# A small memset on POOL behind each gather, in message passing and the last layer

## The reference

```
for _ in range(3):
    msgs = relu(take(h, src) @ W_edge + b_edge)
    agg  = segment_sum(msgs, dst, num_segments=50000)
    h    = relu(concatenate([agg, h]) @ W_agg + b_agg)
x = layernorm(x + h)
```

## Time and profile before

| | us |
|---|---|
| timed runs, median of 3 | 5096.5 (5095.79 to 5099.93) |
| profiled execution, span | 6166.6 |
| of it message passing, two rounds | about 1717 |
| last layer | about 1222 |
| attention | about 1294 |
| feed-forward | about 996 |
| POOL busy over the span | 3168.2 (51%) |
| PE busy over the span | 4568.4 (74%) |

### The profile page before, as it was taken

One profiled execution on the slowest core, in us unless ns is written; L12 is line 12 of the kernel. 1 busy time (PEld: TensorE's weight loads), 2 busy tenths in 40 slices (PEclk: granted clock), 3 DMA queues, 4 the chain that ended last, 5 costly groups with the idle time before them and its releaser, 6 DMA issues. The chain is left out here.

```text
span 6166.6 us, 106939 instructions
## 1 busy us (share of the span) xinstructions
PE 4568.4 (74%) x21995; PEld 2882.5 (47%) x21996; DVE 3657.1 (59%) x12075; ACT 2092.9 (34%) x4610; POOL 3168.2 (51%) x3348
## 2 busy tenths in 40 slices
PE   5666657777767777688888887566666666888887
PEld 3444435555555555555555554344444443333333
DVE  7666643333333333466666655677777776777777
ACT  0222223333333333322323323222222223666665
POOL 1555554444344444333333332666666664888887
PEclk9888878888888888889999998555555556999999
DMA  0333335555545555455665655333333332333333
GB/s 26 128 129 127 124 123 150 149 151 152 152 146 151 149 151 149 144 172 174 187 189 174 187 176 156 86 90 88 92 90 88 90 88 69 107 103 106 104 103 96
DMA packets 690049, 789.03 MB, mean 128 GB/s; under 512 B 145529, under 2 KB 545648, under 8 KB 689900
## 3 DMA queue, kind: packets, MB, share of 16 engines
q1 hardware_dynamic: 577004, 568.56, 28.9%
q0 software_dynamic: 112896, 218.94, 14.0%
HBM read 414.24 MB, written 372.92 MB: 128 GB/s over the span
## 5 line engine op out<-in xcount | busy, mean ns | idle before, releaser
L759 POOL DMA_INDIRECT mp_gathered<-msg_rows,other_idx x784 | 746.7, 952 | 947.8 <-PE bank L776 626.1
L776 PE MATMUL bank<-mp_edge_hot,mp_gathered 128*128 128x256 bf16 x3528 | 606.6, 304 | 279.3 <-issue 227.7
L1076 POOL DMA_INDIRECT ll_gathered<-msg_rows,other_idx x392 | 386.7, 987 | 782.8 <-PE bank L1096 607.7
L525 POOL DMA_INDIRECT by_window<-so_pay,so_pos_i x392 | 395.0, 1008 | 438.1 <-issue 303.9
L1363 POOL DMA_INDIRECT at_kv<-kv_rows,kv_idx x392 | 426.8, 1089 | 343.0 <-DVE at_v_e L1512 236.7
L776 PEld LDWEIGHTS bank<-mp_edge_hot,mp_gathered 128*128 x3528 | 373.4, 106 | 452.1 <-issue 383.9
L879 DVE TENSOR_TENSOR mp_msg_out<-mp_rest,mp_msg_out 128x256 bf16<-128x256 f32 x392 | 166.6, 425 | 649.1 <-ACT mp_msg_out L837 379.7
L1647 POOL DMA_INDIRECT ff_agg<-at_rows,last_idx x392 | 414.1, 1056 | 97.2 <-issue 89.7
L1365 POOL DMA_INDIRECT at_q<-q_rows,node_idx x392 | 390.0, 995 | 123.4 <-issue 123.4
L1143 PE MATMUL bank<-ll_weights,ll_x_cols 128*128 128x512 f32 x784 | 424.1, 643 | 4.5 <-issue 4.4
L824 ACT ACTIVATE mp_h_out<-bank,mp_b_agg 128x256 f32<-128x256 f32 x392 | 186.1, 475 | 702.3 <-PE bank L794 400.8
(11 more groups left out here) (247 smaller groups left out, 10008.7 us busy)
## 6 DMA issues: line engine op xcount, KB each, us to landing
msg_rows<-mp_msg_out SPq DMA_DIRECT2D x392, 192.0 KB
mp_h_in<-h_cols SPq DMA_DIRECT2D x392, 128.0 KB
h_cols<-mp_h_out SPq DMA_DIRECT2D x392, 128.0 KB
kv_rows<-ll_proj SPq DMA_DIRECT2D x98, 512.0 KB
msg_rows<-so_msg_out SPq DMA_DIRECT2D x98, 384.0 KB
h_cols<-so_h_out SPq DMA_DIRECT2D x98, 256.0 KB
ll_h_in<-h_cols SPq DMA_DIRECT2D x196, 128.0 KB
x_rows<-ll_x_b SPq DMA_DIRECT2D x98, 256.0 KB
```

What stands on the lines that cost most here:

```text
L525: pool.indirect_dma_start(core.by_window, bass.IndirectOffsetOnAxis(ap=pos_i[k][:, t:t + 1], axis=0), pay[k][:, t, :], None, bounds_check= ...
L759: pool.indirect_dma_start(gathered[:, r * PARTS * D:(r + 1) * PARTS * D], None, core.msg_rows[layer % 2], bass.IndirectOffsetOnAxis(ap=cor ...
L776: product = nc.tensor.matmul(agg_bank[k], gathered[:, bass.ds(at + d * D, D)], hot, start=(first and d == 0), stop=True, skip_group_check= ...
L1076: pool.indirect_dma_start(gathered[:, r * PARTS * D:(r + 1) * PARTS * D], None, core.msg_rows[(LAYERS - 1) % 2], bass.IndirectOffsetOnAxis ...
```

## The change

`Core` gets a tile `pause` of 128 x 256 f32 in SBUF. Behind each gather of `message_passing` and of `last_layer`, POOL writes zeros into it. Nothing reads the tile. So that two writes of the same tile are ordered, each memset raises a semaphore by one and waits for the count of the memsets before it. The other stages, whose gathers are written in other lines, stay as they are.

```
+        self.pause = ctx.enter_context(nc.sbuf_tensor("pause", [P, 2 * P], F32))
...
                             pool.indirect_dma_start(gathered[:, r * PARTS * D:(r + 1) * PARTS * D], None, core.msg_rows[layer % 2],
                                                     bass.IndirectOffsetOnAxis(ap=core.other_idx[:, i:i + 1], axis=0)).then_inc(g_in[q], 16)
+                            reached(pool, paused, layer * NT + i)
+                            pool.memset(core.pause[:, :], 0.0).then_inc(paused, 1)
                             if i % TOLD == TOLD - 1:
...
                     pool.indirect_dma_start(gathered[:, r * PARTS * D:(r + 1) * PARTS * D], None, core.msg_rows[(LAYERS - 1) % 2],
                                             bass.IndirectOffsetOnAxis(ap=core.other_idx[:, i:i + 1], axis=0)).then_inc(g_in[q], 16)
+                    reached(pool, paused, i)
+                    pool.memset(core.pause[:, :], 0.0).then_inc(paused, 1)
```

More of the change, by code:

```diff
@@ L650, in message_passing @@
         msg_out = sb("mp_msg_out", [P, MSGS, 2, PARTS, D], BF16)
-        wts, tabs_ok = core.sem("mp_weights_in"), core.sem("mp_place_tables")
+        wts, tabs_ok, paused = core.sem("mp_weights_in"), core.sem("mp_place_tables"), core.sem("mp_paused")
         h_ld, h_st = ([core.sem(f"mp_{n}{r}") for r in range(RING)] for n in ("h_loaded", "h_stored"))
@@ L952, in last_layer @@
         x1_cols, x1_b2, proj = many(2, "x1_cols", [D, GR]), many(2, "x1_b2", [P, T, D]), many(2, "proj", [P, T, NPJ])
+        paused = core.sem("ll_paused")
         wts, parts_c, zero_ok, tabs_ok = (core.sem("ll_" + n) for n in ("weights_in", "parts_chain", "zeros_ready", "place_tables"))
```

## The result

| | us |
|---|---|
| before, median of 4 (three of them as above) | 5097.35 |
| changed kernel, median of 4 | 5225.28 |
| ratio, 95% interval | 1.0252 (1.0239 to 1.0264) |
| profiled execution of the changed kernel, span | 5220.0 |

The change costs 128 us where 243 were forecast. The same kernel before takes about 5090 us in some groups of runs (the short groups) and about 6000 us in others (the long groups), and each experiment is compared with the runs of before in its own group, by their medians, which two single executions far off (one of 5626 us of `e2_mp_only` and one of 19159 us of before) hardly touch.

A forecast was written before the change was run, and what follows sets the result against it. The prediction took POOL's gather cycle, 12.4 us a chunk, to pace message passing in the timed run. 5096.5 + 240 (message passing) + 3 (last layer) = 5340 us; range 5090 to 5450 us.

The forecast's parts named there:

- POOL paces message passing in a timed run: Message passing: the timed run sits at or near POOL's floor, so memsets add 240 us; forecast 5340 us, chance 0.62.
- The floor of 12.4 us a chunk: Message passing: POOL's own cycle for eight gathers when nothing holds it, 12.4 us, rising to 14.85 us with memsets.
- the hidden case: Rival, message passing: POOL stays hidden, only the starts of three layers cost, 9 us at most; about 5100 us, chance 0.15.
- a longer chunk before: Message passing: if the timed chunk before is 14.1 us, only 0.75 us of the memsets shows per chunk, 74 us.
- The price of a memset: On POOL behind each gather: one memset costs 0.35 us, with ends of 0.24 and 0.6 us.
- the turn between a gather and an ordinary instruction: On POOL: the loss in turning from gather to ordinary instruction and back, 0.08 us, read from feed-forward.
- Seven of eight exposed, the last under the landing wait: Message passing, per chunk: seven memsets lengthen POOL's cycle by 2.45 us; the eighth lies in the 2.5 us landing wait.
- The last layer: Last layer: PE needs 18.4 us for four windows, above POOL's 14.85 us, so memsets are hidden except 3 us.
- the 3 us of the start: Last layer: only the first chunk's eight memsets show, 8 x 0.35 = 3 us.
- a budget of stalls: Trace against timed run: stalls of 456 us in message passing and at most 319 us in the last layer, of 1070 us.
- The dearer memset: Rival: a memset costs more behind a gather than in feed-forward, 0.6 us and over; about 5500 us, chance 0.10.
- The thinner stalls: Rival, message passing: gathers set apart from 1.25 to 1.6 us stall PE less; about 4990 us, chance 0.13.

The follow-up runs named there:

- e2_mp_only: Changed kernel with the memsets of the last layer left out, so behind each gather of message passing only: 5222.03 us against 5089.98 (1.0258), short group.
- e3_ll_only: Changed kernel with the memsets of message passing left out, so behind each gather of the last layer only: 5089.98 us (0.9998), short group.
- e4_one_column: Changed kernel with each memset cut to one column per partition: 6024.12 us (1.0044), long group.
- e1_before_again: The kernel before, unchanged, traced again (the second trace): 5091.36 us against 5089.98 (1.0003), short group.
- the late telling: With 512-column memsets in both stages; in message passing POOL tells PE of the previous chunk's second half after the new chunk's second gather: 5145.98 us (1.0121).
- e12_wide_again: Changed kernel with memsets of 512 columns instead of 256, run a second time: 5629.56 us (0.9395), long group.
- e9_change_again: The changed kernel, run once more against the kernel before: 5212.72 us against 5084.75 (1.0252), short group.

## Why the prediction was right, and where it was off

**POOL paces message passing in a timed run: right, in the short groups.** The floor of 12.4 us a chunk is 12.44 us in the second trace. All the cost is in message passing (132 us in `e2_mp_only`, 128 of them between its first and last gather, none in `e3_ll_only`), PE's waits for POOL there went from 143.5 to 254.0 us, and the memsets cost less where a wait covers them. The measured time lies between the forecast and the hidden case, inside the range. But the lowest price that the prediction allowed, 0.24 us, gives about 5263 us at POOL's floor. The range took in 5225 us only because its lower end came from other cases (a longer chunk before, 5170 us, and hidden memsets, 5090 us), and that is luck in part.

**The price of a memset: the term that was mis-sized, by nearly half.** The forecast had 0.35 us; the gathers moved apart by 0.19 (1.25 to 1.44). The memset's length was right (0.31 forecast, 0.33 measured). What failed in it is the turn between a gather and an ordinary instruction. The prediction took 0.08 us from feed-forward, where the gather itself is longer (1.10 us). Here the gather stays at 0.95 us and the gap ahead of it shrinks from 0.30 to 0.16 us, so 0.14 us of each memset lies in a gap that was there before. The lower end, 0.24 us, was too high as well. `e4_one_column` shows the same with the other sign: a memset of 0.11 us costs nothing, since gap and memset together are the old 0.30 us.

**Seven of eight exposed, the last under the landing wait: right.** The cycle went from 12.27 or 12.44 us to 13.57 us, by 1.1 to 1.3 us; seven times 0.19 is 1.33. And 98 times 1.1 to 1.3 us is 111 to 127 us, beside the 128 measured. So with the measured price the forecast's own sum comes out.

**The last layer: right.** 17.61 us a chunk without and 17.62 with the memset (`e1_before_again` and `e3_ll_only`); the 3 us of the start are not to be seen there. In the change's own trace the last layer's gathers take 865.5 us against 862.8, so about as much.

**Why the first trace was 1070 us longer: wrong in part.** The prediction said that its stalls don't happen in a timed run. They did not in the runs that were timed then, but they do in whole groups of runs: the timed runs of before take 5981 to 6016 us there. The Trainium skill ("Runtime: NRT & Kernel Launch", the section on the preamble and postamble) has the profile's total some 6 us above the reported time. Here span and time of one and the same execution are 5089.3 and 5091.15 us before and 5220.0 and 5222.3 us after: also close, but the span, from the first to the last instruction, is the shorter by about 2 us. So such a gap doesn't explain the 1070 us; the first trace and the first timed runs were of two different kinds. It was luck for the forecast that the timed runs were of the short kind, for it holds there, and what the change does in a long group was not measured.

The placing of the timed run at POOL's floor was argued by a budget of stalls, 456 us in message passing and at most 319 us in the last layer. Between the two traces of before, the gathers of message passing span 1671 and 1300 us and those of the last layer 1121 and 863 us, so the true shares are 371 and 258 us. The prediction left open what makes the rest of the 1070 us. Most of it is in two stages that it did not weigh: the sorting (707 and 519 us from its first gather to its last) and the attention (1281 and 1076 us), 393 us together.

**The rivals.** Hidden POOL is out for the short groups: the gathers moved apart by 0.19 us and the time grew by 128 us. The dearer memset, 0.6 us and over, is out, since one costs 0.19 us. The thinner stalls, given 0.13, are seen in the long groups: with 1.25 us between gathers they stay, with 1.65 us they are gone and the time falls by 6%. At what distance between the two they begin to go, and so what the change itself would do in a long group, stays open. One reading behind that rival was loose: in feed-forward not every gather comes 2.7 us behind the last, for two of them start at 5607.43 and 5608.84 us, 1.41 us apart.

## What to carry to other kernels

Before a wait is read as slack, lay the profiled span beside the timed median; if they are a fifth apart, trace again, for the two may be different kinds of execution with different bounds, as they were here. A queue's own cycle (its instructions, its gaps, and the wait that it always meets) is the bound to add to, and new work is priced against the gap that it can fill: 0.33 us of memset cost 0.19 us between gathers, and nothing at 0.11 us. A pause between gathers has no fixed sign: memsets of 256 columns cost 2.5% in short groups, where the gathers are on the path, and memsets of 512 columns took 6% off in long ones, where TensorE stalled under gathers 1.25 us apart. Neither was run in the other kind of group, but for the 512 columns with the late telling, which cost 1.2% in a short one.

## What the runs showed of the hardware

The kernel before took 5076 to 5100 us in three groups of runs and 5981 to 6016 us in two, the two executions named above aside, and each experiment took the level of its group. It isn't one device or the other: of the groups behind the first, the one of `e1_before_again` (short) and that of `e12_wide_again` (long) ran on the same chip, and so did those of `e9_change_again` (short) and `e4_one_column` (long). The words "what must be a device" in the expectation of `e9_change_again` are not borne out.

Feed-forward is alike in both kinds (963 us from the first to the last gather in both `e1_before_again` and `e4_one_column`); sorting, message passing, the last layer and attention are not. What is longer in the long kind is idle time, above all: between the two traces of before, DVE is busy for 3657 and 3642 us, ACT for 2093 and 2083 us, and the packets of queues q0 and q1 take 42.9% of 6166.6 us and 52.3% of 5089.3 us, which is 2646 and 2662 us for each DMA engine. So the packets aren't slower. PE's matmuls are busy for 4568 and 4208 us, at a granted clock of 0.79 and 0.85. In message passing and the last layer PE, ACT and DVE idle in the long kind while POOL's gathers follow one another at 1.25 us; with 1.65 us between them the last layer runs at nearly the short group's pace in a long group. Sorting and attention, which have no memset, stay long in `e12_wide_again` too (692 and 1173 us beside 519 and 1076 us).

Memsets on POOL lengthen one kind of DVE's instructions. The building of `mp_edge_hot`, a TENSOR_SCALAR in bf16, has a mean of 354 ns without them (`e1_before_again`), 420 ns with 256 columns (the change) and 528 ns with 512 (`e12_wide_again`), while the TENSOR_TENSOR into `mp_msg_out` stays at 425 and 426 ns. Why one and not the other was not tried.

What ties the stalls to the gathers' distance was not found: the descriptors, the memory, and what else runs on the device were not tried apart. A kernel with the wide memset in the last layer alone was not run. By `e3_ll_only` (with 256 columns) it would cost nothing in a short group; an estimate from the last layer's spans in a long one (1229 and 986 us) is a saving of some 240 us.
